# Recurrence of a graph and feed-forward kernel: pad and root of two groups in one GpSimd step, unit rows split two and two

## The reference

```python
def step(h, _):                      # 30 times, on layernorm(x)
    h = h + 0.01 * jnp.tanh(h)
    h = h * jax.nn.sigmoid(h)
    h = _layernorm(h, ln_w, ln_b)    # mean and variance over 128 features of a row
    h = jnp.einsum('bsc,dc->bsd', h, W) + b
    return (h, None)
...
x = x + _L0_gnn_ref(_layernorm(x), adj, ...)
x = x + _L0_ffn_ref(_layernorm(x)[None], ...)[0]
```

## Time and profile before

| what | value |
|---|---|
| median of 3 runs | 1408.65 us (1407.69 to 1413.42) |
| the profiled execution's own time | 1410.62 us |
| its span, first to last instruction | 1408.8 us |
| busy: PE, DVE, ACT, POOL | 92%, 90%, 81%, 53% |
| GpSimd roots of the recurrence, line 1257 | 240 of 1019 ns, 244.4 us |
| GpSimd units, line 1263 | 240 of 405 ns, 97.1 us |
| GpSimd pads, line 1254 | 240 of 205 ns, 49.2 us |
| VectorE bn_stats, line 1182 | 480 of 421 ns, 182.1 us |
| VectorE adds, line 1175 | 232 of 684 ns, 158.8 us |
| VectorE units, line 1188 | 240 of 476 ns, 114.2 us |

### The profile page before, as it was taken

The page is one execution under the profiler, slowest core; times in us unless marked ns, Lnnn a source line. Parts: engine busy times, 40 slices in busy tenths (PEclk is TensorE's granted clock), DMA queues, the critical chain, the costliest instruction groups (busy, mean ns, idle before and its releaser), DMA issues. The chain is left out here.

```text
span 1408.8 us, 27557 instructions
## 1 busy us (share of the span) xinstructions
PE 1290.5 (92%) x7723; PEld 798.0 (57%) x7723; DVE 1263.1 (90%) x2294; ACT 1142.6 (81%) x1806; POOL 743.4 (53%) x975
## 2 busy tenths in 40 slices
PE   5599999999977999999999987999999999899895
PEld 4444444444436888888888874444444444433664
DVE  7699999999988999999999998899999999966763
ACT  5687777777777999999999987788888888677773
POOL 4210544345449999999999995004223444126654
PEclk9899999999998999999999997999999999999997
DMA  7055555555529991000000000555555555104330
GB/s 266 1 195 193 187 203 203 184 192 195 202 77 344 335 327 46 0 0 0 0 0 0 0 0 1 172 187 209 188 200 192 195 206 185 55 16 138 92 94 23
DMA packets 65798, 186.76 MB, mean 133 GB/s; under 512 B 4515, under 2 KB 47539, under 8 KB 49234
## 3 DMA queue, kind: packets, MB, share of 16 engines
q1 hardware_dynamic: 62738, 179.74, 37.5%
q0 software_dynamic: 3008, 6.37, 1.3%
HBM read 145.51 MB, written 41.49 MB: 133 GB/s over the span
## 5 line engine op out<-in xcount | busy, mean ns | idle before, releaser
L1046 PEld LDWEIGHTS r_p_y<-w_ffn,r_z_t 128*128 128x128 f32 x1920 | 254.9, 193 | 6.5
L1046 PE MATMUL r_p_y<-w_ffn,r_z_t 128*128 128x128 f32 x1920 | 254.7, 276 | 0.0
L1257 POOL TENSOR_TENSOR r_stat<-r_stat,minus_half 128x4 f32<-128x4 f32 x240 | 244.4, 1019 | 18.8
L153 POOL TENSOR_TENSOR b_variance<-x_stats,inv_d 128x4 f32<-128x4 f32 x8 | 54.7, 6834 | 290.9 <-DVE x_stats L144 290.9
L802 ACT ACTIVATE b_prob<-b_p_s,shift,g_unit 128x1024 f32<-128x1024 f32 x128 | 154.3, 1206 | 57.4 <-PE b_p_s L718 57.4
L802 ACT ACTIVATE a_prob<-a_p_s 128x1024 f32<-128x1024 f32 x128 | 131.0, 1024 | 64.2 <-PE a_p_s L718 64.1
L1182 DVE BATCH_NORM_STATS2 r_parts<-r_z 128x6 f32<-128x256 f32 x480 | 182.1, 421 | 0.0
L885 DVE SCALAR_TENSOR_TENSOR a_prob<-adj_rows,a_prob 128x1024 f32<-128x1024 int32 x128 | 160.0, 1250 | 18.5 <-ACT a_prob L802 16.8
L885 DVE SCALAR_TENSOR_TENSOR b_prob<-adj_rows,b_prob 128x1024 f32<-128x1024 int32 x128 | 156.9, 1226 | 19.0 <-ACT b_prob L802 18.8
L1175 DVE SCALAR_TENSOR_TENSOR r_h<-r_tanh,r_p_y 128x512 f32<-128x512 f32 x232 | 158.8, 684 | 3.3
L891 DVE TENSOR_TENSOR a_lo<-a_prob,a_hi 128x1024 f16<-128x1024 f32 x128 | 160.3, 1253 | 0.0
(11 more groups left out here) (287 smaller groups left out, 2975.3 us busy)
## 6 DMA issues: line engine op xcount, KB each, us to landing
adj_rows<-in_adj_t SPq DMA_DIRECT2D x128, 1024.0 KB, 4.8
sorted_rows<-blank SPq DMA_DIRECT2D x7, 4160.0 KB
x_got<-sorted_rows SPq DMA_DIRECT2D x46, 130.0 KB, 2.2
sorted_rows<-blank SPq DMA_DIRECT2D x1, 4290.0 KB
x_rows<-in_x SPq DMA_DIRECT2D x4, 512.0 KB, 8.9
wd_raw<-in_wd SPq DMA_DIRECT2D x1, 2048.0 KB, 10.3
late<-in_late SPq DMA_DIRECT2D x1, 756.0 KB
out_x<-b_rows,x_to_row POOLq DMA_INDIRECT x46, 2.6
```

The costliest lines, as they stand in the source:

```text
L1046: last = nc.tensor.matmul(out[:, D * t:D * t + D], z_t[g % R][:, P * t:P * t + P], k.w_ffn[:], start=False, stop=(t == TPC - 1), skip_grou ...
L1257: nc.gpsimd.tensor_tensor(stat[g][:, 1, :], stat[g][:, 0, :], k.minus_half[:], ALU.pow)\
```

## The change

GpSimd pads and roots two groups in one instruction each (`pad`, `root`, eight columns), behind the statistics of the second, from step 1 on; in step 0 it still takes one group at a time. `parts` and `stat` become one tile for two groups. The unit rows are split two tiles to VectorE and two to GpSimd in every group, none to ScalarE. The first two steps are written out (`opening`) and the loop begins at step 2: in step 0 the units of VectorE come 2 slots behind and the copies of ScalarE 3, in place of 4 and 6, and step 1 leaves out what step 0 has already done. The last chunk's rows are finished within the first four slots, `invert_rows` for them stands on GpSimd behind group 2, and VectorE makes the start rows of group 7 with four `normalised` after slot 5 (`last_rows`); `begin` no longer calls `invert_rows`, and the first attention calls it just ahead of `begin`.

```diff
     def begin(self, pool, c):
-        invert_rows(k, self.x_stats, pool, c)
...
                     if is_a:
+                        invert_rows(k, x_stats, pool, c - 1)
                         first_rows.begin(pool, c - 1)
...
-    DVE_TILES, POOL_TILES = (2, 3) * (G // 2), (1,) * G
-    act_groups = [g for g in range(G) if DVE_TILES[g] + POOL_TILES[g] < TPC]
+    DVE_TILES, POOL_TILES = (2,) * G, (2,) * G
     UNIT_LAG, LEAVE_LAG = 4, 6
+    FIRST_LAG = 2
...
-        parts = [k.sb(f"r_parts{g}", [P, TPC // 2, 6], F32, ctx) for g in range(G)]
-        stat = [k.sb(f"r_stat{g}", [P, 2, TPC], F32, ctx) for g in range(G)]
+        parts = [k.sb(f"r_parts{g}", [P, 2, TPC // 2, 6], F32, ctx) for g in range(0, G, 2)]
+        stat = [k.sb(f"r_stat{g}", [P, 2, 2, TPC], F32, ctx) for g in range(0, G, 2)]
...
-                if g in act_groups:
-                    pe.wait_ge(s["unit_act_ready"], len(act_groups) * i + act_groups.index(g) + 1)
...
-                        act.wait_ge(first_rows.s["centred"], 2 * G)
+                        act.wait_ge(s["last_ready"], 1)
...
-            stages = ((0, tanhs), (1, silus), (UNIT_LAG, unit), (LEAVE_LAG, leave))
+            stages = ((0, tanhs), (1, silus), (LEAVE_LAG, leave))
+            def opening(i):
+                for g in range(G):
+                    n = G * i + g
+                    for lag, first_lag, stage in ((0, 0, tanhs), (1, 1, silus), (LEAVE_LAG, FIRST_LAG + 1, leave)):
+                        if i == 0 and g >= first_lag:
+                            stage(n - first_lag, g - first_lag)
+                        elif i > 0 and n - lag >= G - first_lag:
+                            stage(n - lag, (g - lag) % G)
...
+            def last_rows():
+                dve.wait_ge(first_rows.x_stats["inverting"], 3 * G)
+                for t in range(TPC):
+                    last = normalised(k, z_unit[G - 1][:, D * t:D * t + D], G - 1, t)
+                last.then_inc(s["last_ready"], 1)
+            last_parts = ((), (0, 1, 2, 3), (4,), (5, 6))
+            def opening(i):
+                for g in range(G):
+                    n = G * i + g
+                    add_tanh(n, g)
+                    if i == 0 and g < len(last_parts):
+                        for part in last_parts[g]:
+                            first_rows.finish(dve, CHUNKS - 1, part)
+                    if n > 0:
+                        measure(n - 1, (g - 1) % G)
+                    if i == 0 and g >= FIRST_LAG:
+                        unit(n - FIRST_LAG, g - FIRST_LAG)
+                    elif i > 0 and n - UNIT_LAG >= G - FIRST_LAG:
+                        unit(n - UNIT_LAG, (g - UNIT_LAG) % G)
+                    if i == 0 and g == G - 3:
+                        last_rows()
...
-            peeled(dve, STEPS_KERNEL, step)
+            opening(0)
+            opening(1)
+            with dve.Fori(2, STEPS_KERNEL) as i:
+                step(i, False)
...
+            def pad(n, g, count):
+                mine = slice(g % 2, g % 2 + count)
+                pool.wait_ge(s["measured"], n + count)
+                nc.gpsimd.tensor_tensor(stat[g // 2][:, 0, mine, :].rearrange("p g (a b) -> p (g a) b", b=2),
+                                        parts[g // 2][:, mine].rearrange("p g a s -> p (g a) s")[:, :, 2:6:3],
+                                        k.eps_sum[:, 0:2].unsqueeze(1).broadcast_to([P, count * TPC // 2, 2]), ALU.add)\
+                    .then_inc(s["padded"], count)
+            def root(n, g, count):
+                mine = slice(g % 2, g % 2 + count)
+                pool.wait_ge(s["padded"], n + count)
+                nc.gpsimd.tensor_tensor(stat[g // 2][:, 1, mine, :], stat[g // 2][:, 0, mine, :],
+                                        k.minus_half[:].unsqueeze(1).broadcast_to([P, count, TPC]), ALU.pow)\
+                    .then_inc(s["rstd_ready"], count)
...
             def step(i, first):
                 for g in range(G):
-                    rstds(G * i + g, g)
+                    if first or g % 2 == 0:
+                        pad(G * i + g, g, 1 if first else 2)
+                        root(G * i + g, g, 1 if first else 2)
                     unit(G * i + g, g)
-                    if first and g == 3:
-                        first_rows.begin(pool, CHUNKS - 1)
+                    if first and g == 2:
+                        invert_rows(k, first_rows.x_stats, pool, CHUNKS - 1)
```

More of the change, by code:

```diff
@@ L999, in recurrence @@
         p_len, p_mean, p_top = p_y[0], p_y[1], p_y[2]
-        names = ("y_ready", "tanh_ready", "h_ready", "z_ready", "measured", "padded", "rstd_ready",
-                 "unit_ready", "unit_act_ready", "unit_pool_ready", "t_ready", "zt_ready", "f_ready", "rows_hi", "ft_ready",
+        names = ("last_ready", "y_ready", "tanh_ready", "h_ready", "z_ready", "measured", "padded", "rstd_ready",
+                 "unit_ready", "unit_pool_ready", "t_ready", "zt_ready", "f_ready", "rows_hi", "ft_ready",
                  "hi_ready", "lo_ready", "g_ready", "squared", "mov_hi", "mov_lo", "len_ready", "top_ready", "mean_step",
@@ L1118, in silus @@
                 nc.scalar.activation(z[g][:], h[g % R][:], ACT.Silu).then_inc(s["z_ready"], 1)
[L1120 to L1127, removed]
             def leave(n, g):
@@ L1137, in step @@
                     for lag, stage in stages:
-                        if not (first and g < lag):
-                            stage(G * i + g - lag, (g - lag) % G)
+                        stage(G * i + g - lag, (g - lag) % G)
             def features(c):
@@ L1157, in queries @@
                                      bias=k.m_g[:, D:D + 1]).then_inc(s["mov_hi"], 1)
-            peeled(act, STEPS_KERNEL, step)
+            opening(0)
+            opening(1)
+            with act.Fori(2, STEPS_KERNEL) as i:
+                step(i, False)
             for j in range(G + TURN_LAG + 1):
@@ L1181, in measure @@
                 for i in range(TPC // 2):
-                    last = nc.vector.bn_stats(parts[g][:, i, :], tiles(z[g])[:, 2 * i:2 * i + 2, :].rearrange("p t d -> p d t"))
+                    last = nc.vector.bn_stats(parts[g // 2][:, g % 2, i, :], tiles(z[g])[:, 2 * i:2 * i + 2, :].rearrange("p t d -> p d t"))
                 last.then_inc(s["measured"], 1)
@@ L1188, in unit @@
                 nc.vector.tensor_tensor(tiles(z_unit[g])[:, 0:own, :], tiles(z[g])[:, 0:own, :],
-                                        stat[g][:, 1, 0:own].unsqueeze(2).broadcast_to([P, own, D]), ALU.mult).then_inc(s["unit_ready"], 1)
+                                        stat[g // 2][:, 1, g % 2, 0:own].unsqueeze(2).broadcast_to([P, own, D]), ALU.mult).then_inc(s["unit_ready"], 1)
             stages = ((0, add_tanh), (1, measure), (UNIT_LAG, unit))
-            last_parts = ((0, 1), (2, 3), (4,), (5,), (6,))
+            def last_rows():
[19 more added lines that the diff above has]
+                        last_rows()
             def step(i, first):
@@ L1263, in unit @@
                 nc.gpsimd.tensor_tensor(tiles(z_unit[g])[:, own, :], tiles(z[g])[:, own, :],
-                                        stat[g][:, 1, own].unsqueeze(2).broadcast_to([P, POOL_TILES[g], D]),
+                                        stat[g // 2][:, 1, g % 2, own].unsqueeze(2).broadcast_to([P, POOL_TILES[g], D]),
                                         ALU.mult).then_inc(s["unit_pool_ready"], 1)
```

## The result

The changed kernel takes 1402.82 us (median of 10 runs, 1398.72 to 1406.18) against 1409.93 for the kernel before beside it. The ratio is 0.9942, interval 0.9924 to 0.996: 7 us faster by the medians, 8 by the ratio, where 28 were forecast. The time lies inside the stated range of 1374 to 1432, but outside the likeliest case's own 1375 to 1390. The profiled execution spans 1401.5 us.

What follows compares the result with a forecast made beforehand. GpSimd was taken to bound the loop at 1.72 us a group, VectorE after the change at 1.61: 25.9 us gained, plus 1 each for opening and end, 27.9 in all, giving 1382 us, range 1374 to 1432.

Steps and rivals of the forecast that it cites:

- likeliest case: Whole kernel: short root of eight columns, VectorE bounding the loop; 1375 to 1390 us, chance 0.50.
- X: GpSimd's step for a root of eight columns: between 1.09 and 1.90 us, taken near the lower end, up to 1.5.
- the price of the meetings: Loop, colliding VectorE and GpSimd instructions: GpSimd comes second, loses up to 0.6 us a pair, 3.1 under 3.22, cost 0.
- the ends: Opening and end of the stretch around the loop: 1 us gained in each, from 3 gained to 2 lost and 0 to 2.
- The pad's step: GpSimd in the loop: one pad for two groups steps 0.28 us, four more columns costing nothing visible.
- a VectorE unit over 0.42: Sign in the loop's profile: a VectorE unit longer than 0.42 us would make the prediction wrong.
- Rival B: Loop, faster by less: X of 1.5 to 1.75, or 1.90 without collisions; 15.6 us gained, 1391 with the ends; chance 0.15.
- rival C: Loop, no change: collisions eat the gain, period 3.38 to 3.5 us, 1408 us; chance 0.08.
- The rest of the sum: Loop steps per pair besides the root: VectorE 3.22 us, TensorE 3.08, ScalarE 2.96, GpSimd's two units 1.12.
- a loop's branch costs: Loop branches, with no slack left over them: the reason for saying 1382 us where the sum gave 1380.8.
- Rival A: Loop, slower: root costs by the column, X = 1.90, GpSimd bounds; +21 us, 1430, at worse +56, 1465; chance 0.27.
- covered up to X of about 2: Loop: a pair's root waits for the second group's bn_stats; VectorE's unit two slots (3.2 us) later hides that wait.

Runs made afterwards that it cites:

- half-root run: The changed kernel, but behind step 0 only the first group of each pair is rooted, four columns instead of eight: 1382.95 us, ratio 0.9801.

## Why the prediction was wrong

**The step that failed** has two terms, and the second rests on the first. The first is the one that the prediction called its weakest: "I take an X near the lower end, up to 1.5". The root of eight columns steps 1.71, three quarters of the way from the lower end, 1.09, to the upper, 1.90. The reasoning was a comparison with a multiply, whose 128 extra columns cost 0.20 us; a root's column costs 0.157 us, a hundred times a multiply's 0.0016. Four columns were no small load. The prediction had the better comparison beside it: pad and root of the same shape differ by 0.81 us, which it doubled for its upper end. Nothing in the rows said how much of that is paid once per call; by the measured line 0.63 of it comes again with four more columns, and some 0.2 doesn't. The Trainium skill (GPSIMD Engine Reference, section 3.1) describes a loop over the elements; the prediction cited it for the rival, and the measured line agrees, with the 0.37 us fixed part beside it.

The second term is the price of the meetings: "GpSimd is the one that comes second: cost 0". By the prediction's own sum an X of 1.71 alone costs nothing: GpSimd's pair is then 1.40 + 1.71 = 3.11, still under VectorE's 3.22. But the zero had been worked out with the lowest X only, 2.49 + 0.6 = 3.1. With the 1.5 that the prediction allowed, the same 0.6 gives 3.5, and with 1.71 it gives 3.7: both over 3.22. The pad's 0.3 alone would fill the room at 1.5 (3.2) and pass it at 1.71 (3.4). Nor is GpSimd always second: in the changed kernel VectorE's unit starts behind GpSimd's and pays 0.19 itself. The forecast needed the short root not for GpSimd's own work but for the room that its delays take.

**What took its place.** By the steps GpSimd has 0.34 + 1.71 + 1.12 = 3.17 and VectorE 3.21; the measured 3.38 is 0.17 above the longer. VectorE's unit falls into GpSimd's first unit and is 0.19 longer, and GpSimd's two units take 0.2 more: each delays the other. That neither has a gap in which it could get out of step is how I explain that the meeting comes back in every pair; the run with one GpSimd tile less, where a gap and no meeting are seen, agrees with it. The loop gained 8.3 us where 25.9 were forecast: these 17.6 us are most of what is missing, the ends most of the rest. In the half-root run GpSimd's units are as long as in the changed kernel (1.36), but there it has 0.38 to spare, and "cost 0" held. The pad's step, 0.34 for 0.28, was a small miss. The prediction's own sign, "a VectorE unit over 0.42", came: 0.59.

**Rival B** has the X that was measured, "X between 1.5 and 1.75, or 1.90 with the collisions avoided", chance 0.15. But it gave 1391 and a period of 3.31; the 3.38 is the lower edge of rival C, "collisions eat the gain", chance 0.08, which gave 1408. The kernel lies between the two.

**The rest of the sum held, in part by luck.** With the root at 1.09 the kernel takes 28.4 us less than the kernel before beside it, where 27.9 were forecast. The steps read from the rows (0.68, 0.33, 0.60 on VectorE; 0.56 for a two-tile GpSimd unit; TensorE and ScalarE under the bound) all came back. But the loop gave 28.8 us for 25.9, and the rest of the span 0.7 for 2. The sum's last term, 1.2 us for a loop's branch costs, no run shows: in the half-root run, nearly every pair takes 3.19 to 3.21, across the loop's ends too.

**Rival A** (slower, +21 us) needed X = 1.90; at 1.71 GpSimd stays just under VectorE. Its mechanism is real and is the bound of the run with the tiles alone.

**The chain.** The prediction called the item's wait "covered up to X of about 2". At the measured X of 1.71 no such wait bounds the changed kernel. But with VectorE's first unit a slot later and no meetings left the period was 3.52 where VectorE's own work is 3.21, so the cover was under a slot.

**The ends.** I forecast 1 us each. The way to item 8 grew from 18.7 to 20.4 us though more units are done by then; the drain shrank by 1.3, and VectorE's wait for the row statistics from 1.9 to 1.2 us:

```profile
838.39 1.14 DVE L166 TENSOR_SCALAR r_z<-x_rows,x_stats,rstd 128x128 f32<-128x128 f32 x4 [1.21 <-POOL rstd L158]
```

In the opening VectorE now waits for GpSimd's roots, as its units follow two slots behind:

```profile
434.19 0.43 DVE L1189 TENSOR_TENSOR a_start<-r_z,r_stat 128x256 f32<-128x256 f32 x1 [2.15 <-POOL r_stat L1287]
```

**The direction and the chances.** Faster was forecast at 0.65 and came; the size was under a third of the forecast.

**What the change is worth, part by part.** Pairing pad and root: 14 us. The two-and-two tiles on top of it: 6 us lost. The opening: 0. The parts don't simply add: without the pairing the same tiles lose 102 us.

## What to carry to other kernels

When an instruction's cost per element isn't in the trace, compare it with another operation of the same shape: what it costs beyond that one may well grow with the width (here 0.63 of 0.81 us did), and a run of a few widths settles it. A cost put at nothing because an engine has room must be worked out again for every value that the engine's own work may take. Two engines whose instructions hold each other up need slack on one of them; filling both to within a few per cent of the same period cost more here (0.17 us of 3.2) than leaving a tile on VectorE or ScalarE, which had more to do. And a trace in which two engines have no gaps isn't a proof that their work fills the period: look for one instruction with two lengths.

## What was not expected of the hardware

- A GpSimd root that has run for some tenths of a microsecond doesn't hold VectorE up: VectorE units that start 0.42 us into a root of eight columns take 0.40 us (600.57 against 600.15), though the root runs 1.64.
- Two runs of units that start together delay each other by 0.4 us on both engines (1.16 for 0.75, 1.61 for 1.18). A single VectorE unit that starts with 0.31 us of a 0.61 us GpSimd unit left lost 0.19. The Trainium skill (SBUF — State Buffer, "Who interferes with whom") calls the port pair that the two engines share an exclusive lock. Turns taken instruction by instruction would agree with the 0.4 us. But the 0.19 is less than the 0.31 that a block to the end of the record would cost, and the root above, long as it is, delays nothing at all, so here a block for a record's whole length isn't what is measured. No run shows that the shared ports are the cause: the runs show who is delayed, when, and by how much.
- The cost of a root is a straight line in its columns from 4 to 16 to a hundredth of a microsecond, and 10.54 us for 64, where the line gives 10.4.
